# Two plain chunks first in each layer, the normalization later in VectorE's order, and the gathers split five and five, in a CIN and MLP kernel

## The reference

```python
e = stack([tbl_f[ids[:, f]] for f in range(39)], axis=1)        # 512 x 39 x 16
prev = e
for k in range(3):                                              # 128 units each
    z = einsum('bmd,bhd->bdmh', e, prev)                        # products of fields
    t = einsum('bdc,co->bdo', z.reshape(b, 16, -1), w[k]) + bs[k]
    t = transpose(t, (0, 2, 1))
    t = t / sqrt(sum(t * t, axis=(-2, -1), keepdims=True))      # norm of a sample
    logit.append(t)
    prev = t
z = sum(concatenate(logit, axis=1), axis=-1)                    # 512 x 384
h = concatenate([z, dense_ctx], axis=1)
y = relu(relu(h @ W_top1 + b_top1) @ W_top2 + b_top2) @ W_top3
```

## Time and profile before

| | |
|---|---|
| median of 3 runs | 1323.89 us (1323.67 to 1325.28) |
| the profiled execution | 1321.28 us |
| its span, first to last instruction | 1319.4 us |
| TensorE busy, whole span | 1170.5 us (89%) |
| VectorE busy | 984.2 us (75%) |
| GpSimd busy | 912.1 us (69%) |
| ScalarE busy | 113.7 us (9%) |
| mean granted TensorE clock | 0.962 |
| moved by DMA | 204.31 MB, mean 155 GB/s |

### The profile page before, as it was taken

How to read it: one execution, slowest core, us unless ns; L and a number is a source line. 1 busy time by engine, 2 the same in 40 slices (tenths; PEclk the granted TensorE clock), 3 DMA queues, 4 the chain that set the end, 5 groups by cost and what they waited for, 6 DMA issues and landing times.

```text
span 1319.4 us, 21655 instructions
## 1 busy us (share of the span) xinstructions
PE 1170.5 (89%) x7868; PEld 581.0 (44%) x7868; DVE 984.2 (75%) x836; ACT 113.7 (9%) x219; POOL 912.1 (69%) x614
## 2 busy tenths in 40 slices
PE   0888989999898998979899897999989799898989
PEld 0334545444444444435344453544445354444443
DVE  2596878788587878858788686878868687887771
ACT  0010100101000010100101000010101001010102
POOL 5565877777676786767678586777858677655660
PEclk9889989999899999989999999998999999899989
DMA  6946265463635645364463626546362654537010
GB/s 174 389 123 252 59 223 150 145 205 98 212 85 181 191 135 185 89 205 131 145 212 105 226 58 222 150 145 201 104 236 60 203 168 145 193 101 245 1 42 1
DMA packets 104409, 204.31 MB, mean 155 GB/s; under 512 B 49131, under 2 KB 52075, under 8 KB 104390
## 3 DMA queue, kind: packets, MB, share of 16 engines
q1 hardware_dynamic: 97610, 202.52, 46.8%
q0 software_dynamic: 5120, 1.29, 1.0%
q10 hardware_dynamic: 1660, 0.25, 0.1%
HBM read 201.72 MB, written 2.30 MB: 155 GB/s over the span
## 4 chain that ended last, share of the span: by engine, by line
issue 29%; POOL 29%; PE 27%; DVE 7%; DMA 2%; SPq 2%; POOLq 1%; ACT 1%; DVEq 0%; ACTq 0%
POOL sums L278 12%; PE acc L690 9%; POOL gathered L243 9%; PE mix_ps L690 8%; PE acc L676 8%; POOL sums L281 6%; DVE z L543 4%; DMA w_sb<-in_w 2%; POOL rows_of L237 1%; SPq L351 1%; ACT cross L442 1%; PE t_ps L782 1%; DVE inv L589 0%; DVE u L552 0%; DVE v L556 0%
## 5 line engine op out<-in xcount | busy, mean ns | idle before, releaser
L543 DVE TENSOR_TENSOR z<-t_ps,xb 128x2048 f32<-128x2048 f32 (+1 forms) x352 | 708.2, 2042 | 100.3 <-PE acc L690 79.8
L281 POOL TENSOR_TENSOR sums<-z,sums 128x1024 f32<-128x1024 f32 x192 | 454.5, 2367 | 15.1
L278 POOL TENSOR_TENSOR sums<-z 128x512 f32<-128x512 f32 x192 | 250.6, 1305 | 285.2 <-DVE z L543 276.9
L676 PE MATMUL acc<-z,w_sb 128*64 128x512 f32 x1920 | 434.3, 596 | 7.4 <-DVE z L543 7.4
L690 PE MATMUL mix_ps<-sums,s_sb 128*64 128x256 f32 x1536 | 299.3, 391 | 28.8 <-POOL sums L281 25.8
L690 PE MATMUL acc<-z,w_sb 128*64 128x256 f32 x768 | 244.9, 402 | 78.8 <-DVE z L543 78.8
L676 PEld LDWEIGHTS acc<-z,w_sb 128*64 128x64 f32 x1920 | 138.2, 138 | 243.0 <-issue 229.3
L690 PE MATMUL mix_ps<-z,w_sb 128*64 128x256 f32 x768 | 244.8, 402 | 0.0
L690 PE MATMUL acc<-z,s_sb 128*64 128x256 f32 x768 | 243.0, 400 | 0.0
L690 PE MATMUL p_ps<-z,w_sb 128*64 128x256 f32 x768 | 243.0, 400 | 0.0
L243 POOL DMA_INDIRECT gathered<-in_table,rows_of x160 | 180.5, 1128 | 65.8 <-issue 48.3
(11 more groups left out here) (73 smaller groups left out, 413.8 us busy)
## 6 DMA issues: line engine op xcount, KB each, us to landing
xb<-xt SPq DMA_DIRECT2D x80, 768.0 KB, 5.8
xb<-xq SPq DMA_DIRECT2D x96, 512.0 KB, 4.5
xb<-xt SPq DMA_DIRECT2D x96, 512.0 KB, 5.7
xr<-xt SPq DMA_DIRECT2D x144, 156.0 KB
x<-xt SPq DMA_DIRECT2D x45, 78.0 KB
gathered<-in_table,rows_of POOLq DMA_INDIRECT x160, 4.1
xr<-xt SPq DMA_DIRECT2D x32, 78.0 KB
xt<-gathered SPq DMA_DIRECT2D x16, 72.0 KB, 2.3
```

What stands on the lines that cost most here:

```text
L278: nc.gpsimd.tensor_tensor(t2, t3, b11, ALU.add).then_inc(sums_ready, 1)
L281: nc.gpsimd.tensor_tensor(t41, b2, t2_twice, ALU.subtract).then_inc(sums_ready, 1)
L543: nc.vector.tensor_tensor(z[:, at:at + n, :], t_ps[k - 1][:, :].rearrange("p (a n) -> p a n", a=1).broadcast_to([P, n, N]), xb[:, XB_ROW[c ...
L676: last = nc.tensor.matmul(acc[k][o, :], w_sb[k][:, D_FIELD + 3 * d + r, o], z[:, at + r, :], start=(c == 0 and r == 0), stop=(c == NCH - 1 ...
```

## The change

The order of the chunks goes from D P P D P P D P P D D to D D P P D P P D P P D, so a layer starts with two plain chunks and ends with one. The places of the ring follow from it (three chunks back now at the second product of layer 1, for instance, where it was four). In VectorE's order, `normalize` goes from behind the product of c4 of layer 2 to behind that of c9, with `scale0` right behind it; the two `norm_sums` of layer 2 stand two products later; `shared_sums` and `add_shared` of the tile before stand one product later. In TensorE's order `add_partitions` goes from behind c4 to behind c6. Of the ten gathers, five stand in each gap. The number, kind and size of the instructions stay as they are.

```diff
-CHUNKS = [("D", 0), ("P", 0), ("P", 1), ("D", 1), ("P", 2), ("P", 3), ("D", 2), ("P", 4), ("P", 5), ("D", 3), ("D", 4)]
+PLAIN_IN = [3, 3, 0, 0, 3, 0, 0, 3, 0, 0, 3]
+
+def chunks():
+    out, field, p = [], PAIRED, 0
+    for n in PLAIN_IN:
+        out.append(("D", field, n) if n else ("P", p, 4))
+        field, p = field + n, p + (not n)
+    return out
+
+CHUNKS = chunks()
...
                         if k == 1 and c == LAST_P and gathers:
-                            gather(i + 2, range(0, 8))
+                            gather(i + 2, range(0, 5))
                         if k == 2 and c == LAST_P and gathers:
-                            gather(i + 2, range(8, GROUPS))
+                            gather(i + 2, range(5, GROUPS))
...
-            sp.wait_ge(z_ready, chunks_to(TILES - 1, 2, 1))
+            sp.wait_ge(z_ready, chunks_to(TILES - 1, 2, 2))
...
                     products(i, 1, c)
-                    if c == 0 and not first:
+                    if c == 1 and not first:
                         shared_sums(i - 1, 2)
-                    if c == 1 and not first:
+                    if c == 2 and not first:
                         add_shared(i - 1, 2)
...
                     products(i, 2, c)
-                    if c == 1:
+                    if c == 3:
                         norm_sums(1, i)
-                    if c == 2 and not last:
+                    if c == 4 and not last:
                         norm_sums(0, i + 1)
-                    if c == 4:
+                    if c == 9:
                         normalize(i + 1, *layers_of(first, last))
-                    if c == 5 and not last:
-                        scale0(i + 1)
+                        if not last:
+                            scale0(i + 1)
...
-                layer(i, 2, range(0, 5), first)
+                layer(i, 2, range(0, 7), first)
                 add_partitions(i + 1, *layers_of(first, last))
-                layer(i, 2, range(5, NCH), first)
+                layer(i, 2, range(7, NCH), first)
```

More of the change, by code:

```diff
@@ L53 @@
 PAIRS = PAIRED // 2
-CHUNKS = [("D", 0), ("P", 0), ("P", 1), ("D", 1), ("P", 2), ("P", 3), ("D", 2), ("P", 4), ("P", 5), ("D", 3), ("D", 4)]
+PLAIN_IN = [3, 3, 0, 0, 3, 0, 0, 3, 0, 0, 3]
[6 more added lines that the diff above has]
+CHUNKS = chunks()
 NCH = len(CHUNKS)
[L56 to L59, removed]
+XB_ROW = [sum(n for _, _, n in CHUNKS[:c]) for c in range(NCH + 1)]
+FIRST_P = PLAIN_IN.index(0)
+LAST_P = NCH - 1 - PLAIN_IN[::-1].index(0)
 NP = PAIRS // 2
 STEPS = 2 * NCH
-D_FIELD = PAIRED
 RING = 14
@@ L70, in ring @@
     for s in range(STEPS):
-        n = ROWS_OF[CHUNKS[s % NCH][0]]
+        n = CHUNKS[s % NCH][2]
         if pos + n > RING:
@@ L77, in ring @@
     for s in range(STEPS):
-        n = ROWS_OF[CHUNKS[s % NCH][0]]
+        n = CHUNKS[s % NCH][2]
         for d in range(1, STEPS + 1):
             r = (s - d) % STEPS
-            if at[r] < at[s] + n and at[s] < at[r] + ROWS_OF[CHUNKS[r % NCH][0]]:
+            if at[r] < at[s] + n and at[s] < at[r] + CHUNKS[r % NCH][2]:
                 back.append(d)
@@ L354, in load_chunk @@
             def load_chunk(i, c):
-                t, d = CHUNKS[c]
+                t, d, rows = CHUNKS[c]
                 plain = xt[bass.ds(i, 1), :, :].rearrange("a m n -> (a m) n")
@@ L358, in load_chunk @@
                 if t == "D":
-                    load_rows(c, plain, D_FIELD + 3 * d, 3, XB_ROW[c])
+                    load_rows(c, plain, d, rows, XB_ROW[c])
                 else:
@@ L532, in products @@
                 s = (k - 1) * NCH + c
-                at, n = RING_AT[s], ROWS_OF[CHUNKS[c][0]]
+                (kind, _, n), at = CHUNKS[c], RING_AT[s]
                 if c == 0:
@@ L536, in products @@
                 if k == 1:
-                    dve.wait_ge(xb_loaded[c], (16 if n == 3 else 32) * (i + 1))
+                    dve.wait_ge(xb_loaded[c], (16 if kind == "D" else 32) * (i + 1))
                 back = RING_BACK[s]
@@ L671, in direct @@
             def direct(i, k, c):
-                d = CHUNKS[c][1]
+                _, field, n = CHUNKS[c]
                 at = RING_AT[(k - 1) * NCH + c]
-                for r in range(3):
+                for r in range(n):
                     for o in (LEFT, RIGHT):
-                        last = nc.tensor.matmul(acc[k][o, :], w_sb[k][:, D_FIELD + 3 * d + r, o], z[:, at + r, :],
-                                                start=(c == 0 and r == 0), stop=(c == NCH - 1 and r == 2),
+                        last = nc.tensor.matmul(acc[k][o, :], w_sb[k][:, field + r, o], z[:, at + r, :],
+                                                start=(c == 0 and r == 0), stop=(c == NCH - 1 and r == n - 1),
                                                 skip_group_check=True)
```

## The result

The changed kernel takes 1250.29 us (median of 4 runs, 1250.1 to 1251.33) against 1323.78 us of the kernel before, a ratio of 0.9446 with a 95% interval of 0.943 to 0.9462. That is 5.5% less, and 34 us more than forecast, just outside the range (1198 to 1248).

The account below looks back on a forecast made before the run. TensorE was taken to bound the kernel. First tile 120.5, 13 tiles 919, the last two 70.4 and 68.0, long gather waits 6, and 27.7 at the end gave span 1211.7, or 1216 us as median; range 1198 to 1248.

Parts of the forecast that it names:

- The stall of 4.62 us: TensorE standing still behind add_partitions in layer 2, waiting for c5's product, once a tile; forecast to go.
- The first tile's T: Start of ScalarE's copy behind layer 2 in the first tile; forecast at 120.5, against 125.9 before.
- U to T: Stretch from ScalarE's copy behind layer 1 to that behind layer 2; forecast 37.85 us, against 45.48.
- the wait at c3: TensorE waiting for GpSimd's second sum at layer 2's pair chunk c3; forecast 0.45 us lost.
- what comes in the wait's place: Normalization and scale0 on VectorE ahead of c10's product, once the root is ready; 2.6 us.
- The cover at c10: VectorE's lead over TensorE for c10's product behind the normalization; 1.9 us, and if gone TensorE waits the difference.
- T to U: Stretch from ScalarE's copy behind layer 2 to that behind the next layer 1; forecast 32.9 us, 0.8 more than before.
- the gathers' long waits: Occasional long waits inside GpSimd's gathers, three of them behind layer 2 at about 2 us; 6 us in all.
- Rival 1: GpSimd takes the place: half of the 12 pair chunks lose 0.4 us more, giving 1252; chance 0.10.
- Rival 2: The clock falls at layer starts, where TensorE waits briefly, two falls a tile, giving 1277; chance 0.07.
- Rival 3: The five gathers behind layer 2 land too late, holding mix_rows and the pair sums, giving 1369; chance 0.02.
- rival 4: VectorE still waits as long for the root, so the time stays near 1322; chance 0.01.

Follow-up runs that it names:

- experiment 6: Changed kernel with the normalization early again: normalize behind c4, scale0 behind c5, add_partitions behind c4; 1338.51 us.
- experiment 1: Changed kernel with the normalization's results prod and half kept in PSUM instead of SBUF; 1221.09 us.
- experiment 2: Changed kernel with only half of the normalization in PSUM, prod still in SBUF; 1245.35 us.
- experiment 7: Changed kernel with normalize and scale0 one product later, behind c10, everything in SBUF; 1236.32 us.
- experiment 4: Kernel before with only normalize and scale0 behind c8 of layer 2 and add_partitions behind c5; old chunk order, gathers eight and two; 1261.07 us.
- experiment 3: Changed kernel with the gathers split eight and two again; 1266.27 us.
- 5: Changed kernel with prod and half in PSUM and mix_rows behind layer 1's second pair chunk instead of the first; 1208.37 us.
- experiment 8: Kernel before, old chunk order, with later normalization and add_partitions, prod and half in PSUM, gathers five and five, mix_rows one pair chunk later; 1197.19 us.

## Why the prediction missed

**What held.** The stall of 4.62 us and the fall of the clock went, and experiment 6 brings both back. The chain finds the root ready. The first tile's T was at 121.1, forecast 120.5. The gathers behind layer 2 are hidden in a usual tile. U to T: forecast 37.85, measured 37.84. That it fits to 0.01 us is in part luck: the wait at c3 came (0.42 us, 0.6 by the starts, for 0.45), and the one of 0.25 at c6 did not.

**The step that failed** is the one that says what comes in the wait's place: "2.6 us of VectorE time (655.36 to 657.3, and 0.69 for `scale0`)". The term measured 5.6 us. Its durations came from a moment at which GpSimd stood idle: the trace of before has its next addition at 659.67, behind the whole chain. In the new place the chain runs beside GpSimd's two additions for c9, and two of its instructions are held until they end. The cover at c10, 1.9 us by my working, was too small for 3.0 more. The second part of the same step is what a lost cover costs: I had "TensorE would wait the difference, once a tile", and that difference came, 1.0 us, but VectorE has no gap from c10 to the first pair product and hands the delay on, and TensorE loses 1.5 us more at c2. Experiment 1 takes nearly all of the meeting away and leaves the order as it is, and 2.27 of the 2.65 us that I had missed in T to U are back.

Of the other 0.38, half is the same meeting in another place, which the forecast didn't have either. GpSimd's last addition of layer 1 runs beside `products0`, which also reads two SBUF operands, in the changed kernel:

```profile
591.89 4.83 DVE L536 TENSOR_TENSOR xr<-x,xr 117x1024 f32<-117x1024 f32 x2
```

```profile
592.41 3.23 POOL L291 TENSOR_TENSOR sums<-z,sums 128x1024 f32<-128x1024 f32 x1
```

The addition takes 3.23 us for 2.36, in experiment 1 as well, and in both TensorE needs 3.2 us for c9 where it needs 3.02 without a wait. The rest, 0.2 to 0.3 us at c2, was not traced to a cause.

In the sum: 15 x 2.65 = 40 us too little for T to U, 2 for U to T in the last tile (37.65 for 35.8, its cause was not looked for), 6 too much for the gathers' long waits, 1 for both ends, together 37 us of span (1248.5 - 1211.7).

The trace of before had the warning, on both engines, and I did not use it. One is the gather of 2.75 us beside `products0`, which I priced for the gathers and not for VectorE. Others show VectorE and the additions themselves:

```profile
626.21 1.93 DVE L526 TENSOR_TENSOR xr<-x,xr 117x1024 f32<-117x1024 f32 x1
...
628.07 1.22 DVE L526 TENSOR_TENSOR xr<-x,xr 117x1024 f32<-117x1024 f32 x1
```

```profile
624.69 2.37 POOL L281 TENSOR_TENSOR sums<-z,sums 128x1024 f32<-128x1024 f32 x1
...
659.67 1.65 POOL L278 TENSOR_TENSOR sums<-z 128x512 f32<-128x512 f32 x1 [7.78 <-DVE z L543]
```

The first product of `products0` starts while the addition runs (to 627.06) and takes 1.93 us; the second, of the same size, takes 1.22. The addition at 659.67 meets `scale0` (659.51 to 660.20, two SBUF operands) and takes 1.65 us for 1.27. The text ahead of the prediction calls semaphores the only tie between engines. This is a tie without one: no row shows VectorE idle for it, the time stands in the instruction's own duration.

The Trainium skill has the rule in "SBUF — State Buffer", section "SBUF: two separate sides": VectorE and GpSimd share a pair of ports under an exclusive lock, and a VectorE instruction with two SBUF inputs takes part in it against a GpSimd instruction that reads SBUF; who starts first keeps it for the whole instruction. By that rule the two instructions wait for the ends of the two additions, and the traces agree (ends 0.12 and 0.11 us apart, and 0.13 and 0.11 in experiment 2, 0.12 in experiment 7). The forecast did not weigh it.

**The rivals.** Rival 1, GpSimd takes the place, gave 1252, and the time is its time, but not by its mechanism: it had half of the pair chunks of both layers lose 0.4 us to GpSimd's speed, and U to T, with nearly all of layer 2, came out as forecast. That its number fits is luck. Rival 2 did not come: the clock stayed up beside waits of 1.5 us. By what the Trainium skill says of short idle times between groups of matmuls, in "TensorE: Matmul & The Clock Gate", section "A second HAM failure mode: psum-queue depth-cycling", it could have come; this trace doesn't show it (granted clock 1.00 from 561 to 597 us). Rival 3 did not come, and rival 4 neither.

**The parts of the change**, by the runs: the later normalization brings 62.5 us by itself (experiment 4), the split of the gathers 16 (experiment 3), and the new order of chunks takes away 5 us (experiment 3 against 4), 11 (5 against 8), or 14 and more (6 against before, where the split of the gathers is in it as well). In the first two pairs the normalization also has one plain product behind it with the new order and two with the old. Why the order costs is seen in part. With two plain products ahead of the additions, the first pair product is later by one plain product. And with one plain chunk behind the last pair chunk, GpSimd's last addition meets `products0` and takes 3.23 us; in experiment 8 it takes 2.38. Between 5 and 8 a usual tile differs by 0.70 us in T to U and 0.64 in U to T. That this is all of it was not tried.

## What to carry to other kernels

When an instruction is moved, its duration has to be read at a place like its new one: look at what the other engines run there, and whether it shares something with them. For VectorE beside GpSimd's additions, count the instructions with two SBUF operands; keeping one operand in PSUM took 2.8 us out of a chain of 5.6. Go through the whole chain: with one of the two slow instructions changed, the hold moved on to the next that qualifies and the kernel gained 5 us, with both 29. And if a cover is lost, ask where the engine behind it has its next gap; up to there the delay is handed on.

## What the runs showed of the hardware

- A VectorE instruction of 0.26 us took 1.15 to 2.40 us when it read two SBUF operands while a GpSimd addition ran, and ended 0.1 us behind it. With one operand in PSUM it took 0.26 to 0.27, and with two in SBUF and GpSimd idle 0.26 (experiment 6). Where its result went did not matter (experiment 2). A larger one, of 1.22 us, took 1.93 and ended 1.1 us behind the addition (kernel before). It works the other way too: an addition of 2.36 us that came while such an instruction ran took 3.23 (changed kernel) or 2.88 (experiment 1), one of 1.27 took 1.65 (kernel before).
- Waits of 2.1 to 5.4 us come at gathers whose count is a multiple of 29: at 58, 87, 116 and 145 of the kernel before, and at 29, 58, 87 and 145 of the changed one. Number 29 in the first and 116 in the second are the first gathers of their group and show none. What they wait for was not tried.
